# A graph attention kernel on one core: the attention output goes through DRAM two sequences at a time, its quotients come two slots later, and SyncE's queue is put in another order

## The chip, the core and the metric

The kernel runs on one core of a Trainium2 chip. The metric is the device time of one execution in microseconds (us), as the median of repeated runs. The engines named here are PE (TensorE, matrix products), DVE (VectorE), ACT (ScalarE), POOL (GpSimd) and SP (SyncE, which in this kernel issues every DMA). Each engine works through its own list of instructions in order. They meet at semaphores: an instruction that waits for a semaphore holds back all that stands behind it on its engine.

## What is computed

64 sequences of 128 tokens and 384 channels, 12 heads of 32 channels, float32. The reference, cut to its core:

```python
h = jnp.maximum(_layernorm(x, axis=-1), 0.0)
q = _split_heads(h @ Wq + bq); k = _split_heads(h @ Wk + bk); v = _split_heads(h @ Wv + bv)
scores = jnp.einsum('bhqd,bhkd->bhqk', q, k) / jnp.sqrt(HD)
scores = scores + beta * adj[:, None]
scores = jnp.where(adj[:, None] > 0, scores, -9e15)
probs = jax.nn.softmax(scores, axis=-1)
out = jnp.einsum('bhqk,bhkd->bhqd', probs, v)
return x + out.transpose(0, 2, 1, 3).reshape(B, N, D)
```

## The kernel before, in words

Four sequences make a group (`GROUP = 4`, 16 groups). The program is a row of **slots**, one for each sequence of each group, and all engines go through the same slots. Slot s (0 to 3) of a group works on several sequences at once: it projects q and k for the group, computes the scores of sequence a, transposes the probabilities of the sequence before it (e = a - 1), and finishes the output of the one before that (o = a - 2). The middle slots stand in a hardware loop of two groups a turn; the first and last groups are written out. The last six sequences (`F`) are finished in another way, by transposes on PE.

Three tiles are transposed in 32x32 blocks by DVE, which needs the blocks themselves moved between partitions. That is done through DRAM: one DMA writes 128 rows, a second set of four DMAs reads them back block by block. All three ways are on SP:

- the normalised input, two sequences at a time: `xhat_blocks` is written to `xhat_rows` in odd slots (384 KB), and read into `xhat_moved` in even slots by four DMAs;
- the first third of each sequence's probabilities: ACT's four exponentials fill `probs_blocks` (`exponentials_ahead`), SP writes it to `probs_rows` (256 KB) late in the slot, and in the next slot SP reads it into `probs_moved` by four DMAs of 64 KB. DVE then transposes it (`transpose_probs`), and PE multiplies it with v a slot later;
- the output: PE writes it transposed, DVE transposes the blocks into `out_blocks` (`store_outT`), SP writes it to `out_rows` (192 KB) and reads it into `out_moved` by four DMAs of 48 KB. One slot later DVE divides by the softmax's sum (`quotient`, into `y`), POOL adds x, and SP stores `y` to the output.

The order of each engine's work is written by hand in its `slot` function. DVE's in a slot of the loop: reciprocals, the 12 masking passes (`mask`; in slot 0 the next one stands before it), `store_outT`, the hidden state's transpose, `normalise` (xhat), `quotient`, `add_bv` (v), `transpose_probs`, then the statistics, the bias and the low part of the hidden state. SP's is in `slot(z)` of the sync block, and the change rewrites it. `LOADS` says which sequences of x are loaded in which slot, three groups ahead.

Of the kernel before, what the change touches and what calls it, by code (L numbers as in the profile page):

```python
# [29 lines left out]
HEADS = 12  # L30
GROUP = 4
# [10 lines left out]
LOADS = [[0], [1, 2], [3], []]  # L42
# [19 lines left out]
def gnn_attention(nc, x, adj, wq, bq, wk, bk, wv, bv, beta, out):  # L62
# [16 lines left out]
    with ExitStack() as ctx:  # L79
# [54 lines left out]
        rinv = sb("rinv", [P, 2, HEADS])  # L134
# [4 lines left out]
        THREE = KC * HD  # L139
# [53 lines left out]
        out_written = [sem(f"out_written{i}") for i in range(2)]  # L193

        class Slot:
# [14 lines left out]
            def __init__(self, i, off, s):  # L210
# [17 lines left out]
                before = 0 <= 4 * (n - 1) + s - 3 < FIRST_F  # L228
                self.moved, self.turned = [1] * before, [0] * (self.F and self.O and not self.L)
# [55 lines left out]
            def written(self, d):  # L285

                return 4 * self.i + (2 * (self.off - 1) + (self.s - 2 - d) // 2)
# [74 lines left out]
        def _(sp):  # L362
# [33 lines left out]
            def slot(z):  # L396
                if z.R:
                    sp.wait_ge(probs_rows_written, 16 * (z.e + 1))
                    for c in range(HC):
                        came = probs_rows[(z.s - 1) % 2, :, c * FOUR:(c + 1) * FOUR].rearrange("(r p) n -> p r n", r=HC)  # L400
                        goes = probs_moved[c * HD:(c + 1) * HD, (z.s - 1) % 2, :].rearrange("p (r n) -> p r n", r=HC)
                        sp.dma_start(goes, came).then_inc(probs_blocks_moved[(z.s - 1) % 2], 16)  # L402
# [4 lines left out]
                if not (z.static and not 1 <= z.groups(0) <= NG - 3):  # L407
                    if z.s % 2 == 1:
                        sp.wait_ge(xhat_ready, order(z.count(2)) + 1)
                        write_rows(z.s // 2)  # L410
                    if z.s == 2:
                        sp.wait_ge(rows_written[0], 16 * z.groups(0))
                        read_blocks(0)
                if z.M and z.s == 0:
                    sp.wait_ge(rows_written[1], 16 * z.groups(-1))
                    read_blocks(1)
                if z.Q:
                    sp.wait_ge(probs_ready[0], z.a + 1)
                    sp.dma_start(probs_rows[z.s % 2, :, :], probs_blocks[:, :]).then_inc(probs_rows_written, 16)  # L419
                if z.W:  # L420
                    sp.wait_ge(out_rows_written, 16 * (z.o + 1))
                    for b in range(HC):
                        came = out_rows[z.s % 2, :, b * THREE:(b + 1) * THREE].rearrange("(j p) n -> p j n", j=HC)
                        goes = out_moved[b * HD:(b + 1) * HD, z.s % 2, :].rearrange("p (j n) -> p j n", j=HC)
                        sp.dma_start(goes, came).then_inc(out_blocks_moved[z.s % 2], 16)  # L425
                for d in z.moved + z.turned:

                    sp.wait_ge(y_ready, z.o + 1 - d)
                    sp.dma_start(out[bass.ds(z.o - d, 1), :, :].rearrange("b t d -> t (b d)"),  # L429
                                 y[:, (z.s - d) % 2, :]).then_inc(out_written[(z.s - d) % 2], 16)  # L430
# [6 lines left out]
                if not (z.static and z.groups(3) >= NG):  # L437
                    if z.s == 0:


                        sp.wait_ge(stats_ready, z.count(1) + 2)
                    for q in LOADS[z.s]:
                        sp.dma_start(x_ring[:, bass.ds(z.ring(3, q), D)],  # L443
                                     x_v[:, bass.ds(z.groups(3), 1), q, :].rearrange("t g d -> t (g d)")).then_inc(x_loaded[(z.par + 1) % 2], 16)
                if z.L:
                    for m in range(KC):
                        sp.wait_ge(third_ready, m + 1)
                        sp.dma_start(out[z.o, :, m * P:(m + 1) * P], y[:, z.s % 2, m * P:(m + 1) * P]).then_inc(out_written[z.s % 2], 16)
# [3 lines left out]
            sp.wait_ge(out_written[0], 16 * B // 2)  # L452
            sp.wait_ge(out_written[1], 16 * (B // 2 + KC - 1))

        @block.gpsimd
        def _(pool):
# [25 lines left out]
            def slot(z):  # L482
# [11 lines left out]
                for d in z.moved + z.turned:  # L494
# [3 lines left out]
                    nc.gpsimd.tensor_tensor(y[:, z.s % 2 ^ d, :], y[:, z.s % 2 ^ d, :], x_ring[:, bass.ds(at, D)], ALU.add).then_inc(y_ready, 1)  # L498
# [131 lines left out]
        def _(dve):  # L630
# [68 lines left out]
            def store_outT(z):  # L699
                dve.wait_ge(pv_done, z.o + 1)  # L700
                if z.W:
                    if started(z.o):
                        dve.wait_ge(out_rows_written, 16 * z.o)
                    nc.vector.transpose(out_blocks[:, :].rearrange("p (b m d) -> p m b d", b=HC, m=KC),
# [6 lines left out]
            def reciprocals(z):  # L711
                dve.wait_ge(probs_ready[2], z.o + 1)
                if started(z.o - 1):
                    dve.wait_ge(normalised, z.o - 1)
# [347 lines left out]
```

## Time and profile before

| | |
|---|---|
| time before, median of 3 runs | 545.62 us (545.51 to 547.7) |
| the profiled execution's own time | 551.03 us |
| its span, first to last instruction | 548.9 us |
| busy: PE, DVE, ACT, POOL | 92%, 85%, 81%, 23% of the span |
| granted TensorE clock | 0.987 of full speed |
| DMA issues by SP in the output's way through DRAM | 58 writes, 232 reads |

The profile is of one execution. A page gives totals, the other views give instructions in order of time. Rows whose engine reads "SPq" are SP issuing DMAs: the duration is that of the issue, not of the transfer. "Idle before" in square brackets says how long the engine had nothing to do before an instruction and who ended that.

### The profile page before, as it was taken

To read this page: it belongs to the slowest core of one execution; us is meant where nothing else is said; L and a number is where in the kernel's file an instruction comes from. 1 tells how busy PE (TensorE), PEld (TensorE's weight loads), DVE (VectorE), ACT (ScalarE), POOL (GpSimd) and SP (SyncE) were. 2 spreads that over 40 slices of the span, in tenths; PEclk is the share of its full clock that TensorE was granted. 3 is DMA by queue.
4 is the path that set the end of the run, shared out by engine and by line. 5 is a ranking of instruction groups with operands and counts; after the bars stand their busy time and mean duration, and the time that the engine had idled before them with its cause. 6 is when DMAs were issued, how large, how long until landed. Compare 5 with 4: busy or idle time off the path is not lost.

```text
span 548.9 us, 17414 instructions
## 1 busy us (share of the span) xinstructions
PE 507.4 (92%) x5142; PEld 418.8 (76%) x5142; DVE 467.3 (85%) x2323; ACT 443.0 (81%) x1816; POOL 127.0 (23%) x204
## 2 busy tenths in 40 slices
PE   8897989997999989899899989999898998999986
PEld 7676868776878778688787878778786887888774
DVE  5686878978989798898989989898898998887796
ACT  3568596796988969788796988889698897989885
POOL 5412121222222222221222222122222221111121
PEclk9999999999999999999999999999899999999999
DMA  7516466776776777767687776767668566655311
GB/s 244 169 55 197 127 209 204 214 218 204 222 244 180 242 215 220 222 202 217 203 249 217 223 233 211 227 206 242 203 192 252 178 198 201 179 160 161 94 45 59
DMA packets 132840, 106.20 MB, mean 193 GB/s; under 512 B 44464, under 2 KB 121904, under 8 KB 132784
## 3 DMA queue, kind: packets, MB, share of 16 engines
q1 hardware_dynamic: 132784, 105.57, 63.5%
q8 instruction: 21, 0.34, 0.3%
q14 instruction: 35, 0.29, 0.2%
HBM read 55.84 MB, written 49.68 MB: 192 GB/s over the span
## 4 chain that ended last, share of the span: by engine, by line
SPq 38%; PE 19%; DMA 12%; DVE 10%; issue 8%; ACT 3%; DVEq 0%; ACTq 0%
SPq L425 12%; SPq L402 11%; DMA out_rows<-out_blocks 8%; PE G_ps L892 7%; PE S_ps L961 4%; SPq L429 4%; SPq L443 4%; PE S_ps L913 4%; SPq L394 4%; DMA probs_moved<-probs_rows 4%; DVE probs L726 4%; PE PT_ps L945 2%; PE PT_ps L929 2%; ACT probs_blocks L542 2%; SPq L419 1%
## 5 line engine op out<-in xcount | busy, mean ns | idle before, releaser
L527 ACT ACTIVATE probs<-probs,negmax 128x128 f32<-128x128 f32 x532 | 206.0, 397 | 0.0
L726 DVE CUSTOM_DVE_ANT_0 probs<-S_ps,bias 128x128 f32<-128x128 f32 x768 | 165.8, 284 | 14.4 <-PE S_ps L913 14.4
L542 ACT ACTIVATE probs_blocks<-probs,negmax 128x128 f32<-128x128 f32 x236 | 91.9, 393 | 71.9 <-DVE negmax L726 71.8
L498 POOL TENSOR_TENSOR y<-y,x_ring 128x384 f32<-128x384 f32 x63 | 63.9, 1014 | 299.6 <-DVE y L744 299.6
L892 PE MATMUL G_ps<-h_hi,w_hi 128*128 128x512 f32 x288 | 120.1, 417 | 0.0
L892 PE MATMUL G_ps<-h_hi,w_lo 128*128 128x512 f32 x288 | 119.0, 413 | 0.0
L892 PE MATMUL G_ps<-h_lo,w_hi 128*128 128x512 f32 x288 | 117.6, 408 | 0.0
L527 ACT ACTIVATION_READ_ACCUMULATOR probs<-probs,negmax 128x1 f32 x532 | 105.0, 197 | 0.0
L764 DVE STREAM_TRANSPOSE probsT<-probs_moved 128x512 f32<-128x512 f32 x59 | 41.8, 709 | 43.3 <-DMA probs_moved<-probs_rows 43.2
L913 PEld LDWEIGHTS S_ps<-qk 32*128 32x128 f32 x1536 | 50.9, 188 | 33.8 <-issue 32.3
L929 PE MATMUL PT_ps<-probsT,v 128*32 128x128 f32 x1512 | 55.6, 281 | 22.1 <-DVE probsT L764 10.7
L913 PE MATMUL S_ps<-qk 32*128 32x128 f32 x1536 | 63.9, 294 | 11.8 <-DVE h_lo L665 11.4
L550 ACT COPY probsT<-PT_ps 128x512 f32<-128x512 f32 x122 | 64.9, 579 | 6.9 <-PE PT_ps L945 6.3
L892 PEld LDWEIGHTS G_ps<-h_hi,w_hi 128*128 128x128 f32 x288 | 55.2, 192 | 15.1 <-issue 3.6
L945 PE MATMUL PT_ps<-ident,probs 128*128 128x128 f32 x492 | 66.2, 273 | 0.0
L961 PE MATMUL S_ps<-w_hi,h_hi 128*128 128x384 f32 x192 | 65.3, 340 | 0.0
L929 PEld LDWEIGHTS PT_ps<-probsT,v 128*32 128x32 f32 x1512 | 39.1, 111 | 34.3 <-issue 26.7
L892 PEld LDWEIGHTS G_ps<-h_lo,w_hi 128*128 128x128 f32 x288 | 55.1, 191 | 13.0 <-issue 3.2
L961 PE MATMUL S_ps<-w_hi,h_lo 128*128 128x384 f32 x192 | 64.6, 337 | 0.0
L961 PE MATMUL S_ps<-w_lo,h_hi 128*128 128x384 f32 x192 | 64.5, 336 | 0.0
L892 PEld LDWEIGHTS G_ps<-h_hi,w_lo 128*128 128x128 f32 x288 | 55.2, 192 | 11.6 <-issue 2.8
L726 DVE DVE_READ_ACCUMULATOR2_ANT negmax<- 128x1 f32 x768 | 63.8, 83 | 0.1
(60 smaller groups left out, 724.7 us busy)
## 6 DMA issues: line engine op xcount, KB each, us to landing
probs_rows<-probs_blocks SPq DMA_DIRECT2D x59, 256.0 KB, 2.8
probs_moved<-probs_rows SPq DMA_DIRECT2D x236, 64.0 KB, 2.3
out_dram<-y SPq DMA_DIRECT2D x63, 192.0 KB, 2.0
x_ring<-in_x_dram SPq DMA_DIRECT2D x61, 192.0 KB, 3.0
out_rows<-out_blocks SPq DMA_DIRECT2D x58, 192.0 KB, 2.1
out_moved<-out_rows SPq DMA_DIRECT2D x232, 48.0 KB, 2.1
xhat_rows<-xhat_blocks SPq DMA_DIRECT2D x26, 384.0 KB, 2.7
xhat_moved<-xhat_rows SPq DMA_DIRECT2D x104, 96.0 KB, 2.5
```

The lines of the kernel that those rows point to most:

```text
L402: sp.dma_start(goes, came).then_inc(probs_blocks_moved[(z.s - 1) % 2], 16)
L425: sp.dma_start(goes, came).then_inc(out_blocks_moved[z.s % 2], 16)
L498: nc.gpsimd.tensor_tensor(y[:, z.s % 2 ^ d, :], y[:, z.s % 2 ^ d, :], x_ring[:, bass.ds(at, D)], ALU.add).then_inc(y_ready, 1)
L527: last = nc.scalar.activation(p, p, ACT.Exp, bias=negmax[:, e, j * KC + m:j * KC + m + 1], scale=TURN, accum_out=rowsum[:, e, m * HC + j:m ...
L542: last = nc.scalar.activation(blocks[:, j, :, :], probs[:, a, j, 0, :].rearrange("p (c e) -> p c e", c=HC), ACT.Exp, bias=negmax[:, a, j * ...
L550: nc.scalar.copy(probsT[:, m, :], pT_bank(z, m)).then_inc(pT_stored[m], 1)
L726: last = nc.vector.tensor_tensor_reduce(probs[:, a, j, m, :], S_ps[:, j, m * N:(m + 1) * N], bias[(z.par + 1) % 2][:, z.s, :], 1.0, LARGES ...
L892: mm = nc.tensor.matmul(G_ps[:, u % 2, :], pairs[n][0], pairs[n][1], start=(n == 0), stop=(n == len(pairs) - 1))
L913: last = nc.tensor.matmul(S_ps[:, j, m * N:(m + 1) * N], qk_a[rs, m, ts], qk_a[rs, KC + m, ts], start=True, stop=True, tile_position=(j * ...
L929: last = nc.tensor.matmul(outT_ps[j * HD:(j + 1) * HD, m * N:(m + 1) * N], v[:, z.s % 2, h * HD:(h + 1) * HD], probsT[:, h // HC, h % HC * ...
L945: last = nc.tensor.transpose(pT_bank(z, m)[:, j * N:(j + 1) * N], probs[:, (z.s - 1) % 2, j, m, :], ident[:, :])
L961: last = nc.tensor.matmul(v_ps, hh, ww, start=(n == 0), stop=(n == len(pairs) - 1))
```

## The change

Five edits. (1) `out_blocks` and `out_rows` hold two sequences; SP writes and reads them in odd slots alone, so that there are half as many DMAs of twice the size (384 KB written, four reads of 96 KB). (2) The quotient, POOL's addition and the store to the output come two slots after the sequence's `store_outT` instead of one, with four places in `y` and `rinv`; `y` and `out_moved` now lie in `w_raw`, the raw weights' buffer, which is why the names in the lists below read `w_raw`. (3) In a slot SP issues the reads of the probabilities' blocks first, then the loads of x and of adj (`load_ahead`), which stood last; behind them come the ways of xhat, the write of the output pair, the write of the probabilities, the store of y, and the reads of the output pair. (4) x's sequences 2 and 3 of a group are loaded in slot 2, instead of 1 and 2 in slot 1. (5) At the first F slot two quotients fall due.

```diff
-LOADS = [[0], [1, 2], [3], []]
+LOADS = [[0], [1], [2, 3], []]
...
-        out_blocks = sb("out_blocks", [P, D])
-        out_rows = nc.dram_tensor("out_rows", [2, P, D], F32, kind="Internal").ap()
-        out_moved = sb("out_moved", [P, 2, D])
-        y = sb("y", [P, 2, D])
+        SIX = 2 * KC * HD
+        out_blocks = sb("out_blocks", [P, HC * SIX])
+        out_rows = nc.dram_tensor("out_rows", [2, P, HC * SIX], F32, kind="Internal").ap()
+        later = w_raw.rearrange("p k n -> p (k n)")
+        out_moved = later[:, 0:2 * HC * SIX].rearrange("p (i n) -> p i n", i=2)
+        y = later[:, 2 * HC * SIX:2 * HC * SIX + GROUP * D].rearrange("p (i n) -> p i n", i=GROUP)
...
-                before = 0 <= 4 * (n - 1) + s - 3 < FIRST_F
-                self.moved, self.turned = [1] * before, [0] * (self.F and self.O and not self.L)
+                first_f = n == NG and s == 0
+                self.moved = [2] * (not self.F and 4 * (n - 1) + s - 4 >= 0) + [2, 1] * first_f
+                self.turned = [0] * (self.F and self.O and not self.L)
...
             def slot(z):
                 if z.R:
                     sp.wait_ge(probs_rows_written, 16 * (z.e + 1))
...
                         sp.dma_start(goes, came).then_inc(probs_blocks_moved[(z.s - 1) % 2], 16)
-                if z.W:
-                    sp.wait_ge(outT_stored, z.o + 1)
-                    sp.dma_start(out_rows[z.s % 2, :, :], out_blocks[:, :]).then_inc(out_rows_written, 16)
+                load_ahead(z)
                 if not (z.static and not 1 <= z.groups(0) <= NG - 3):
...
+                if z.W and z.s % 2 == 1:
+                    sp.wait_ge(outT_stored, z.o + 1)
+                    sp.dma_start(out_rows[1 - z.s // 2, :, :], out_blocks[:, :]).then_inc(out_rows_written, 16)
                 if z.Q:
                     sp.wait_ge(probs_ready[0], z.a + 1)
                     sp.dma_start(probs_rows[z.s % 2, :, :], probs_blocks[:, :]).then_inc(probs_rows_written, 16)
-                if z.W:
-                    sp.wait_ge(out_rows_written, 16 * (z.o + 1))
+                for d in z.moved + z.turned:
+                    sp.wait_ge(y_ready, z.o + 1 - d)
+                    place = (z.s - 2 - d) % GROUP
+                    sp.dma_start(out[bass.ds(z.o - d, 1), :, :].rearrange("b t d -> t (b d)"), y[:, place, :]).then_inc(out_written[place], 16)
+                if z.W and z.s % 2 == 1:
+                    sp.wait_ge(out_rows_written, 16 * (z.pairs_written() + 1))
                     for b in range(HC):
...
-                for d in z.moved + z.turned:
...
-                if z.T and z.s == 1:
...
-                    for q in LOADS[z.s]:
...
             def store_outT(z):
                 dve.wait_ge(pv_done, z.o + 1)
                 if z.W:
-                    if started(z.o):
-                        dve.wait_ge(out_rows_written, 16 * z.o)
+                    if z.s % 2 == 0 and started(z.pairs_written()):
+                        dve.wait_ge(out_rows_written, 16 * z.pairs_written())
```

SP's list in the program, in the loop, from slot 1's write of the probabilities to slot 2's reads of them. Before (L419 is the write, L402 the reads, L425 the output's reads, L443 the loads of x):

```order
L419 DMA probs_rows<-probs_blocks 128x512
L425 DMA out_moved<-out_rows 32x4x96 x4
L429 ISA
L429 DMA out_dram<-y 128x384
L435 ISA
L435 DMA adj_in<-in_adj_dram 128x4x128
L443 ISA
L443 DMA x_ring<-in_x_dram 128x384
L443 ISA
L443 DMA x_ring<-in_x_dram 128x384
L398 REGISTER_ALU
L402 DMA probs_moved<-probs_rows 32x4x128 x4
```

And of the change, from the write of the output pair that stands just ahead of it:

```order
L440 DMA out_rows<-out_blocks 128x768
L442 REGISTER_ALU
L443 DMA probs_rows<-probs_blocks 128x512
L446 REGISTER_ALU
L448 ISA
L448 DMA out_dram<-w_raw 128x384
L450 ISA
L454 DMA w_raw<-out_rows 32x4x192 x4
L421 REGISTER_ALU
L425 DMA probs_moved<-probs_rows 32x4x128 x4
```

The three loads have left this stretch, and the output's reads (now L454) read what the write at the piece's head has only just brought to DRAM.

The next piece of SP's list, from slot 2's reads of the probabilities to its write of the next ones. Before:

```order
L402 DMA probs_moved<-probs_rows 32x4x128 x4
L406 DMA out_rows<-out_blocks 128x384
L412 REGISTER_ALU
L394 DMA xhat_moved<-xhat_rows 32x4x192 x4
L418 REGISTER_ALU
L419 DMA probs_rows<-probs_blocks 128x512
```

Of the change:

```order
L425 DMA probs_moved<-probs_rows 32x4x128 x4
L416 ISA
L416 DMA x_ring<-in_x_dram 128x384
L416 ISA
L416 DMA x_ring<-in_x_dram 128x384
L432 REGISTER_ALU
L401 DMA xhat_moved<-xhat_rows 32x4x192 x4
L442 REGISTER_ALU
L443 DMA probs_rows<-probs_blocks 128x512
```

The output's write is gone from an even slot, and two loads of x stand ahead of the write of the probabilities. On PE and ACT no instruction moves; on DVE and POOL only the quotient and the addition stand for another sequence, and two of each follow each other in the first F slot.

## Rows read from the trace of the kernel before

**Rows 1.** The page's head and its first part: busy time of each engine.

```profile
span 548.9 us, 17414 instructions
PE 507.4 (92%) x5142; PEld 418.8 (76%) x5142; DVE 467.3 (85%) x2323; ACT 443.0 (81%) x1816; POOL 127.0 (23%) x204
```

**Rows 2.** Waits of the engines, all of the span: us in total, times, longest.

```profile
DVE probsT L764 <- DMA probs_moved<-probs_rows: 43.2, 38, 2.7
```

**Rows 3.** The page's chain that ended last, by line.

```profile
SPq L425 12%; SPq L402 11%; DMA out_rows<-out_blocks 8%; PE G_ps L892 7%; PE S_ps L961 4%; SPq L429 4%; SPq L443 4%; PE S_ps L913 4%; SPq L394 4%; DMA probs_moved<-probs_rows 4%; DVE probs L726 4%; PE PT_ps L945 2%; PE PT_ps L929 2%; ACT probs_blocks L542 2%; SPq L419 1%
```

**Rows 4.** Timeline of DVE, one group of the loop: start, us, instruction, idle before.

```profile
269.50 0.70 DVE L764 STREAM_TRANSPOSE probsT<-probs_moved 128x512 f32<-128x512 f32 x1
...
275.56 0.55 DVE L744 TENSOR_TENSOR y<-out_moved,rinv 128x384 f32<-128x384 f32 x1
...
277.06 0.71 DVE L764 STREAM_TRANSPOSE probsT<-probs_moved 128x512 f32<-128x512 f32 x1 [0.48 <-DMA probs_moved<-probs_rows]
...
286.06 0.71 DVE L764 STREAM_TRANSPOSE probsT<-probs_moved 128x512 f32<-128x512 f32 x1 [1.92 <-DMA probs_moved<-probs_rows]
...
293.33 0.71 DVE L764 STREAM_TRANSPOSE probsT<-probs_moved 128x512 f32<-128x512 f32 x1 [0.21 <-DMA probs_moved<-probs_rows]
...
301.31 0.70 DVE L764 STREAM_TRANSPOSE probsT<-probs_moved 128x512 f32<-128x512 f32 x1
```

**Rows 5.** Timeline of SP in the same group: start, us of issuing, DMA.

```profile
275.97 0.36 SPq L386 DMA_DIRECT2D xhat_rows<-xhat_blocks  x1
276.81 0.32 SPq L419 DMA_DIRECT2D probs_rows<-probs_blocks  x1
277.48 1.82 SPq L425 DMA_DIRECT2D out_moved<-out_rows  x4
...
280.66 0.94 SPq L443 DMA_DIRECT2D x_ring<-in_x_dram  x2
281.72 1.78 SPq L402 DMA_DIRECT2D probs_moved<-probs_rows  x4
283.54 0.43 SPq L406 DMA_DIRECT2D out_rows<-out_blocks  x1
284.08 1.88 SPq L394 DMA_DIRECT2D xhat_moved<-xhat_rows  x4
286.08 0.36 SPq L419 DMA_DIRECT2D probs_rows<-probs_blocks  x1
...
289.62 2.05 SPq L402 DMA_DIRECT2D probs_moved<-probs_rows  x4
...
292.66 0.45 SPq L419 DMA_DIRECT2D probs_rows<-probs_blocks  x1
```

**Rows 6.** Timeline of POOL, slot 1 of the same group.

```profile
276.30 1.02 POOL L498 TENSOR_TENSOR y<-y,x_ring 128x384 f32<-128x384 f32 x1 [4.21 <-DVE y L744]
```

**Rows 7.** The page's DMA issues: count, size, median us from issue to landing.

```profile
probs_rows<-probs_blocks SPq DMA_DIRECT2D x59, 256.0 KB, 2.8
...
xhat_rows<-xhat_blocks SPq DMA_DIRECT2D x26, 384.0 KB, 2.7
xhat_moved<-xhat_rows SPq DMA_DIRECT2D x104, 96.0 KB, 2.5
```

**Rows 8.** Timeline of SP in a slot 1 soon after the start.

```profile
79.42 0.38 SPq L419 DMA_DIRECT2D probs_rows<-probs_blocks  x1
...
85.91 1.78 SPq L402 DMA_DIRECT2D probs_moved<-probs_rows  x4
```

**Rows 9.** Timeline of SP in the first slot 1 after the loop.

```profile
405.04 0.42 SPq L419 DMA_DIRECT2D probs_rows<-probs_blocks  x1
...
411.35 1.86 SPq L402 DMA_DIRECT2D probs_moved<-probs_rows  x4
```

**Rows 10.** Windows: busy us of each engine, clock, DMA share, GB/s.

```profile
105.00:398.00 293.00, 274.77 (x2828) 227.12 (x2827) 261.12 (x1308) 246.95 (x1021) 70.67 (x109) 0.99 0.73 219
...
452.00:484.00 32.00, 30.36 (x320) 25.39 (x319) 27.13 (x137) 28.33 (x119) 4.36 (x5) 1.00 0.63 191
```

More of the change, by code:

```diff
@@ L192, in gnn_attention @@
         third_normalised, third_ready = sem("third_normalised"), sem("third_ready")
-        out_written = [sem(f"out_written{i}") for i in range(2)]
+        out_written = [sem(f"out_written{i}") for i in range(GROUP)]
         class Slot:
@@ L394, in read_blocks, with load_ahead @@
                     sp.dma_start(goes, came).then_inc(blocks_moved[pair], 16)
[L396 to L402, printed above, removed]
-                if z.W:
-                    sp.wait_ge(outT_stored, z.o + 1)
-                    sp.dma_start(out_rows[z.s % 2, :, :], out_blocks[:, :]).then_inc(out_rows_written, 16)
[L407 to L419, printed above, removed]
-                if z.W:
-                    sp.wait_ge(out_rows_written, 16 * (z.o + 1))
[L422 to L425, printed above, removed]
-                for d in z.moved + z.turned:
-                    sp.wait_ge(y_ready, z.o + 1 - d)
-                    sp.dma_start(out[bass.ds(z.o - d, 1), :, :].rearrange("b t d -> t (b d)"),
-                                 y[:, (z.s - d) % 2, :]).then_inc(out_written[(z.s - d) % 2], 16)
+            def load_ahead(z):
                 if z.T and z.s == 1:
@@ L444, in slot @@
                                      x_v[:, bass.ds(z.groups(3), 1), q, :].rearrange("t g d -> t (g d)")).then_inc(x_loaded[(z.par + 1) % 2], 16)
+            def slot(z):
+                if z.R:
+                    sp.wait_ge(probs_rows_written, 16 * (z.e + 1))
+                    for c in range(HC):
+                        came = probs_rows[(z.s - 1) % 2, :, c * FOUR:(c + 1) * FOUR].rearrange("(r p) n -> p r n", r=HC)
+                        goes = probs_moved[c * HD:(c + 1) * HD, (z.s - 1) % 2, :].rearrange("p (r n) -> p r n", r=HC)
+                        sp.dma_start(goes, came).then_inc(probs_blocks_moved[(z.s - 1) % 2], 16)
+                load_ahead(z)
+                if not (z.static and not 1 <= z.groups(0) <= NG - 3):
+                    if z.s % 2 == 1:
+                        sp.wait_ge(xhat_ready, order(z.count(2)) + 1)
+                        write_rows(z.s // 2)
+                    if z.s == 2:
+                        sp.wait_ge(rows_written[0], 16 * z.groups(0))
+                        read_blocks(0)
+                if z.M and z.s == 0:
+                    sp.wait_ge(rows_written[1], 16 * z.groups(-1))
+                    read_blocks(1)
+                if z.W and z.s % 2 == 1:
+                    sp.wait_ge(outT_stored, z.o + 1)
+                    sp.dma_start(out_rows[1 - z.s // 2, :, :], out_blocks[:, :]).then_inc(out_rows_written, 16)
+                if z.Q:
+                    sp.wait_ge(probs_ready[0], z.a + 1)
+                    sp.dma_start(probs_rows[z.s % 2, :, :], probs_blocks[:, :]).then_inc(probs_rows_written, 16)
+                for d in z.moved + z.turned:
[4 more added lines that the diff above has]
+                    sp.wait_ge(out_rows_written, 16 * (z.pairs_written() + 1))
+                    for b in range(HC):
+                        came = out_rows[1 - z.s // 2, :, b * SIX:(b + 1) * SIX].rearrange("(j p) n -> p j n", j=HC)
+                        goes = out_moved[b * HD:(b + 1) * HD, 1 - z.s // 2, :].rearrange("p (j n) -> p j n", j=HC)
+                        sp.dma_start(goes, came).then_inc(out_blocks_moved[1 - z.s // 2], 16)
@@ L447, in slot @@
                         sp.wait_ge(third_ready, m + 1)
-                        sp.dma_start(out[z.o, :, m * P:(m + 1) * P], y[:, z.s % 2, m * P:(m + 1) * P]).then_inc(out_written[z.s % 2], 16)
+                        sp.dma_start(out[z.o, :, m * P:(m + 1) * P], y[:, GROUP - 1, m * P:(m + 1) * P]).then_inc(out_written[GROUP - 1], 16)
             slots(sp, slot)
-            sp.wait_ge(out_written[0], 16 * B // 2)
-            sp.wait_ge(out_written[1], 16 * (B // 2 + KC - 1))
+            for place in range(GROUP):
+                sp.wait_ge(out_written[place], 16 * (NG if place < GROUP - 1 else NG + KC - 1))
         @block.gpsimd
@@ L497, in slot @@
                     pool.wait_ge(normalised, z.o + 1 - d)
-                    nc.gpsimd.tensor_tensor(y[:, z.s % 2 ^ d, :], y[:, z.s % 2 ^ d, :], x_ring[:, bass.ds(at, D)], ALU.add).then_inc(y_ready, 1)
+                    place = back % GROUP
+                    nc.gpsimd.tensor_tensor(y[:, place, :], y[:, place, :], x_ring[:, bass.ds(at, D)], ALU.add).then_inc(y_ready, 1)
                 for q in z.stats:
```

38 lines of the change are left out of this document (21 added, 17 removed).

## The prediction

> **What bounds the kernel now.** I read the page's head first: PE is busy 92% of the span and DVE 85% [rows 1]. Neither can be read as full: a busy PE is pipelined work, and DVE has 82 us without work. The list of waits says where most of DVE's idle time lies: 43.2 us in 38 waits, all ahead of the transpose of the probabilities' blocks, for the DMA that moves them [rows 2]. The chain that ended last agrees from the other end: its largest parts are not an engine's work but SP's issues of the output's reads and of the probabilities' reads (L425 and L402, 12% and 11%), and the landing of the output's write (8%) [rows 3]. So the loop is bound by DVE's work and SP's queue in turn, and the change has to be worked out on SP's queue.
>
> The timeline of one group shows how. DVE's five transposes are 7.56, 9.00, 7.27 and 7.98 us apart, and waits of 0.48, 1.92 and 0.21 us stand before the middle three [rows 4]. The group is thus 31.81 us, of which 2.61 are waits and 29.20 DVE's own pace. The timeline of SP explains the long one [rows 5]. Slot 1 writes the probabilities at 276.81. Before it comes to reading them back, SP issues the output's four reads (1.82 us), the store of y, adj, and two loads of x, so that the reads begin at 281.72, 4.91 us after the write. After them come the output's next write and the xhat reads, so that slot 2's write is issued at 286.08, and its reads at 289.62. The transpose follows at 293.33. From slot 1's write to that transpose SP's row takes 4.91 + 4.36 + 3.54 + 3.71 = 16.52 us, and this row, not DVE, sets the pace over slots 2 and 3. From there to the next slot 1's write DVE sets it: no wait stands before the transpose at 301.31.
>
> **What the change removes, adds and moves.** Half of the output's writes and reads go (29 and 116 issues); at 0.46 us each (1.82 for four [rows 5]) that is 67 us of SP's issuing, 1.1 us a slot. Were SP's total the bound, that would be the gain; but only what stands on the 16.5 us row counts. Term by term, with the same group:
>
> (a) Slot 1's write to slot 2's reads, now 4.91. adj and the loads leave it. But the output's reads now wait for a write that is issued just ahead: xhat_rows goes at 275.97, 0.84 before the probabilities' write [rows 5], the output's pair right behind it, 0.4 before. The trace has no such pair. Its nearest row is the xhat write of the same 384 KB, 2.7 us to landing [rows 7]: the lower end. The upper end adds the transfer of the 384 KB ahead of it: the DMA engines moved 219 GB/s at 0.73 of their time [rows 10], so 300 GB/s in full, 1.3 us, together 4.0. I take 3.2, nearer to the lower end, since the median of 2.7 already holds other writes in flight and the one ahead has a start of 0.4. Then the output's reads are issued from 2.8 to 4.7 us after the probabilities' write, and the probabilities' reads at 4.75. Gain 0.16, between 0.65 and a loss of 0.65.
>
> The Trainium skill ("DMA: Bandwidth & Descriptors", Anatomy of one DMA) fits a DMA's time by 2.0 us plus its bytes over 436 KB a us, which gives 2.9 for 384 KB; its fit is for GpSimd's DMAs, the xhat row has 2.7 for SP's. By the page (a) would gain 0.46.
>
> (b) Slot 2's reads to its write, now 4.36: the output's write goes (284.08 - 283.54 = 0.54), two loads of x come in (281.72 - 280.66 = 1.06) [rows 5]: 4.88, a loss of 0.52.
>
> (c) Slot 2's write to slot 3's reads, now 3.54: the output's reads go. What is left is the landing of the write, 2.8 [rows 7]; the store of y fits inside it. 2.85, a gain of 0.69.
>
> (d) The reads to the transpose, 3.71 [rows 4, 5]: unchanged.
>
> Together 16.19 instead of 16.52: 0.33 a group here. In the loop's 293 us DVE was idle for 31.9 [rows 10], over 9.2 groups 3.5 each, 0.9 more than in the group shown; part of that is SP falling behind by more than here, and (a) and (c) then save more, since they end at a landing and not at an issue. I add a quarter of the 0.9 and take 0.55 a group, 5.0 us in the loop.
>
> Outside the loop two slots show a longer (a): 6.49 us soon after the start [rows 8] and 6.31 just behind the loop [rows 9]. At 4.75 they give back 1.7 and 1.6. In the other slots behind the loop, without loads, even slots gain (c) and odd slots lose some of it; PE was idle for only 1.64 us of 32 there [rows 10], so I take 1.0 for the whole part. In the first F slot a second quotient of 0.55 [rows 4] stands on DVE where each step waits for the last: 0.5 lost.
>
> Costed at nothing: slot 1's own transpose loses its wait (0.48), but slot 2's write then still waits for SP, so nothing follows. The wait of 1.92 shrinks by about 1 (the reads no longer land behind adj and loads), and nothing follows for the same reason. The quotient of slot 2 now needs the output's reads: the last is issued at 4.3 after the write and lands 2.5 later by the xhat reads of its new size [rows 7], at 283.6. DVE comes to it about 1.0 us before its transpose [rows 4], at 282.6: a new wait of 1.0 us. It hides inside what is left of the wait for the probabilities, which land at 285.1: quotient and v end at 284.6. POOL's addition ends 1.76 after the quotient's start [rows 4, 6], and its store is issued long before SP would need it in even slots; in odd ones SP waits longer for the output's write anyway.
>
> Sum: 5.0 + 1.7 + 1.6 + 1.0 - 0.5 = 8.8 us of the profiled execution's 551.03, which gives 542.2. That execution was 1% above the median of the runs, 545.62, so the forecast in their terms is 536.9, rounded to 537. The terms' own range is 532 to 542.9.
>
> **The rivals.** *SP's new wait makes it slower.* In odd slots the probabilities' reads are now queued behind a wait for a landing. If the output's pair lands only 4.0 us after its issue, (a) becomes 5.55, a loss of 0.64, and the row 16.99. Slot 3 suffers too. Its write at 292.66 moves 0.4 back behind the output's, and forward by 1.0 with slot 2's earlier transpose; reads 4.75 later and 3.71 to the transpose give 300.5, against DVE's own 300.8: 0.3 of slack, which 0.8 more use up, and 0.5 comes on top. That is 0.97 a group, 9 us, and the two slots outside give 1.6 less: 545.6 + 9 - 3 = 551. The point from which it decides: with (a) at 5.25, a landing of 3.7, the loop gains nothing. For it: two writes of 384 KB and one of 256 KB go out within 1 us. Against: adj and the loads now go out earlier. The Trainium skill (the same page and section) states that DMA engines don't wait on semaphores, the issuing sequencer does; by that rule all that is queued behind the output's reads waits. The 8% of the chain on that landing [rows 3] agrees. Chance 14%.
>
> *Nothing comes of it.* (b) loses what (c) gains, and (a) stands still with a landing of 3.4 to 3.7. Only the slots outside the loop are left, 0 to 3 us: 543 to 547. A repeat of this kernel tells 0.5%, 2.7 us, from no change at best. Chance 22%.
>
> *SP ceases to bind.* If landings shrink with less in flight, so that (a) is 3.5 and (b) and (c) hide, DVE's waits fall to 1 us a group: 2.5 x 9.2 = 23 us and 5 outside: 518. Against: the output's reads alone take 1.9 of (a) and their write 2.7. Chance 6%; and 8% for something between it and my range, 525 to 532, by a landing of 2.7.
>
> **How the numbers follow.** My forecast has 50%. Faster by over 0.5% is 50 + 6 + 8 = 64%, the same 22%, slower 14%. The range reaches from 530 (landing 2.7: 0.5 a group more) to 549 (most of the first rival). It leaves out some 15%.
>
> **What the profile would show.** Right: in the loop the probabilities' reads come 4.5 to 5.0 us after the write in odd slots and 2.8 to 3.0 in slot 2; SP waits for out_rows some 2 us in each odd slot; a new DVE wait before the quotient of slot 2; DVE's wait for probs_moved near 30 us instead of 43.2; groups of 31.3. Wrong: reads at 5.3 or more, or a wait before slot 0's transpose, where none is now; or the quotient's wait so long that the transpose is no longer the last to be served.

## The result, and the profile after

The change made the kernel slower by half a per cent: 549.98 us median of 20 runs (547.62 to 553.56) against 547.38 us of the kernel before, run beside it 20 times (545.17 to 549.6). The ratio is 1.005, with a 95% interval of 1.003 to 1.007. The profiled execution spans 550.4 us, 1.5 more than [rows 1].

The page's head and first part, of the changed kernel:

```profile
span 550.4 us, 17259 instructions
PE 504.8 (92%) x5142; PEld 417.6 (76%) x5142; DVE 469.1 (85%) x2323; ACT 443.3 (81%) x1816; POOL 127.4 (23%) x204
...
DMA out_rows<-out_blocks 14%; SPq L425 12%; DMA probs_rows<-probs_blocks 10%; SPq L454 7%; PE G_ps L906 7%; SPq L401 6%; PE S_ps L975 4%; SPq L416 3%; DMA probs_moved<-probs_rows 3%; PE S_ps L927 2%; DVE probs L737 2%; PE PT_ps L959 2%; PE PT_ps L943 2%; SPq L393 1%; ACT probs L538 1%
```

The engines' work is as it was. The chain has changed: against [rows 3] the issues of the output's reads (now L454) fell from 12% to 7%, but the landing of the output's write rose from 8% to 14%, and the landing of the probabilities' write, which was not in the list, has 10%. SP's issuing was replaced by SP's waiting.

DVE's waits of the changed kernel, all of the span, against [rows 2]:

```profile
DVE probsT L778 <- DMA probs_moved<-probs_rows: 24.2, 30, 2.9
...
DVE w_raw L757 <- issue: 8.8, 11, 1.9
...
DVE out_blocks L715 <- DMA out_rows<-out_blocks: 3.7, 2, 2.7
DVE w_raw L757 <- DMA w_raw<-out_rows: 3.5, 2, 2.1
```

DVE waits 19 us less for the probabilities' blocks. Against that, 12.3 us of waits before the quotient are new (L757; by the program it is the output's reads that it waits for there, also where the view says "issue"), and 3.7 for the output's buffer.

SP's own waits in a stretch of the loop, 144 to 398 us. Before:

```profile
SPq L419 <- ACT probs_blocks L542: 8.6, 14, 1.1
SPq L425 <- DMA out_rows<-out_blocks: 8.5, 14, 1.0
SPq L386 <- DVE xhat_blocks L654: 1.1, 3, 0.4
SPq L406 <- DVE out_blocks L704: 1.0, 1, 1.0
```

After:

```profile
SPq L425 <- DMA probs_rows<-probs_blocks: 26.4, 16, 2.0
SPq L454 <- DMA out_rows<-out_blocks: 20.9, 16, 2.0
SPq L393 <- DVE xhat_blocks L665: 3.4, 2, 2.1
SPq L448 <- POOL w_raw L509: 1.7, 6, 0.4
```

This is the view that tells most. Before, SP waited for ACT's exponentials in 14 slots: there it was on time, and ACT and DVE set the pace. After, there is not one wait for ACT: SP comes late to the probabilities' write in every slot. Yet it spends 47 us waiting for its own writes to land, against 8.5 before, and only 5.1 us waiting for DVE and POOL. What half the issues saved went into those waits, and hardly a slot is left in which SP has time in hand.

The timeline of SP over one group's slots 1 and 2, in the changed kernel, beside [rows 5]:

```profile
309.89 0.36 SPq L393 DMA_DIRECT2D xhat_rows<-xhat_blocks  x1
310.30 0.42 SPq L440 DMA_DIRECT2D out_rows<-out_blocks  x1
310.90 0.38 SPq L443 DMA_DIRECT2D probs_rows<-probs_blocks  x1
...
314.14 1.74 SPq L454 DMA_DIRECT2D w_raw<-out_rows  x4
315.99 1.79 SPq L425 DMA_DIRECT2D probs_moved<-probs_rows  x4
317.99 0.96 SPq L416 DMA_DIRECT2D x_ring<-in_x_dram  x2
319.09 2.03 SPq L401 DMA_DIRECT2D xhat_moved<-xhat_rows  x4
321.34 0.34 SPq L443 DMA_DIRECT2D probs_rows<-probs_blocks  x1
...
324.30 1.75 SPq L425 DMA_DIRECT2D probs_moved<-probs_rows  x4
```

The pair's write goes at 310.30, and SP can read it only from 314.14, 3.8 us later. The probabilities' reads follow at 315.99, 5.09 after their write; the next write is issued 5.35 after that, its reads 2.96 later.

The timeline of DVE in the same group, beside [rows 4]:

```profile
303.66 0.70 DVE L778 STREAM_TRANSPOSE probsT<-probs_moved 128x512 f32<-128x512 f32 x1
310.65 0.71 DVE L778 STREAM_TRANSPOSE probsT<-probs_moved 128x512 f32<-128x512 f32 x1
317.69 0.56 DVE L757 TENSOR_TENSOR w_raw<-w_raw,rinv 128x384 f32<-128x384 f32 x1 [0.33 <-issue]
319.32 0.71 DVE L778 STREAM_TRANSPOSE probsT<-probs_moved 128x512 f32<-128x512 f32 x1 [0.60 <-DMA probs_moved<-probs_rows]
327.69 0.71 DVE L778 STREAM_TRANSPOSE probsT<-probs_moved 128x512 f32<-128x512 f32 x1 [1.31 <-DMA probs_moved<-probs_rows]
335.67 0.70 DVE L778 STREAM_TRANSPOSE probsT<-probs_moved 128x512 f32<-128x512 f32 x1
```

The group takes 32.01 us, where the one of [rows 4] took 31.81. The wait of slot 1 is gone, that of slot 2 is split between the quotient and the transpose, and that of slot 3 has grown from 0.21 to 1.31.

Where the time went, read from three transposes (the first, the twelfth, the forty-fourth of 59) on DVE's timeline. Before:

```profile
39.84 0.70 DVE L764 STREAM_TRANSPOSE probsT<-probs_moved 128x512 f32<-128x512 f32 x1
...
139.63 0.70 DVE L764 STREAM_TRANSPOSE probsT<-probs_moved 128x512 f32<-128x512 f32 x1
...
397.80 0.70 DVE L764 STREAM_TRANSPOSE probsT<-probs_moved 128x512 f32<-128x512 f32 x1
```

After:

```profile
38.67 0.70 DVE L778 STREAM_TRANSPOSE probsT<-probs_moved 128x512 f32<-128x512 f32 x1
...
143.76 0.70 DVE L778 STREAM_TRANSPOSE probsT<-probs_moved 128x512 f32<-128x512 f32 x1
...
399.63 0.70 DVE L778 STREAM_TRANSPOSE probsT<-probs_moved 128x512 f32<-128x512 f32 x1
```

The first eleven slots take 105.1 us instead of 99.8, the next 32 (eight groups of the loop) 255.9 instead of 258.2. So in these two executions the steady loop gained, 0.29 us a group, and the early part lost 5.3.

The granted clock of TensorE has a part in both numbers. In the changed kernel it fell from 2.4 GHz to 1.2 GHz twice ahead of the end of the loop. A window ahead of the first fall, in which PE has no instruction, and one behind it (the number behind POOL's column is the clock):

```profile
132.00:134.00 2.00, 0.00 (x0) 0.00 (x0) 0.00 (x0) 2.00 (x7) 0.00 (x0) 1.00 0.79 267
136.00:142.00 6.00, 5.70 (x36) 4.79 (x35) 5.19 (x31) 1.41 (x8) 0.59 (x1) 0.50 0.54 147
```

TensorE had been idle for 3.33 us before that fall. The slot with the low clock, the last of the early eleven, took 9.75 us; slots of its kind in the loop mostly take 7.98. The kernel before has two such stretches in its early part and two in its 32 slots of the loop, where the change has one and one. The second of its two in the loop lies in the last of the 32 slots, which took 8.86 us, where those of its kind at full clock take 7.98 to 8.33. Up to 0.9 of the 2.3 us gained in the loop can be this.

### The profile page after: what moved, and what is told of

Its sections match the earlier page's. It is cut to its first block, busy times and chain, and to the rows that moved or that the text cites. A ratio compares the mean times of both kernels' runs of the same rounds, so it can differ in the third digit from the quotient of the medians.

```text
span 550.4 us, 17259 instructions
## 1 busy us (share of the span) xinstructions
PE 504.8 (92%) x5142; PEld 417.6 (76%) x5142; DVE 469.1 (85%) x2323; ACT 443.3 (81%) x1816; POOL 127.4 (23%) x204
## 4 chain that ended last, share of the span: by engine, by line
SPq 30%; DMA 27%; PE 18%; DVE 8%; issue 7%; ACT 1%; DVEq 0%
DMA out_rows<-out_blocks 14%; SPq L425 12%; DMA probs_rows<-probs_blocks 10%; SPq L454 7%; PE G_ps L906 7%; SPq L401 6%; PE S_ps L975 4%; SPq L416 3%; DMA probs_moved<-probs_rows 3%; PE S_ps L927 2%; DVE probs L737 2%; PE PT_ps L959 2%; PE PT_ps L943 2%; SPq L393 1%; ACT probs L538 1%
## 5 line engine op out<-in xcount | busy, mean ns | idle before, releaser
L509 POOL TENSOR_TENSOR w_raw<-w_raw,x_ring 128x384 f32<-128x384 f32 x63 | 64.0, 1017 | 312.7 <-DVE w_raw L757 312.7
```

The lines of the kernel that those rows point to most:

```text
L509: nc.gpsimd.tensor_tensor(y[:, place, :], y[:, place, :], x_ring[:, bass.ds(at, D)], ALU.add).then_inc(y_ready, 1)
```

## The experiments

Two theories stood against each other for the loss. **Theory 1**, the landing: the output's pair is written behind xhat's 384 KB, lands late, and SP waits for it in front of the probabilities' reads. **Theory 2**, the order: loads that stood behind the writes now stand ahead of slot 2's write and make it late. Means below are over the eight groups between the twelfth and forty-fourth transpose, from the issue times and landings in each kernel's timeline. Every ratio is to the kernel before, run beside that experiment. Where a time is set against the change, the change's 549.98 us is of another session; the kernel before had medians of 547.32 to 547.99 us in all of them.

**e1, the order alone.** The kernel before, with `LOADS` and SP's loads as in the change:

```diff
-LOADS = [[0], [1, 2], [3], []]
+LOADS = [[0], [1], [2, 3], []]
...
                         sp.dma_start(goes, came).then_inc(probs_blocks_moved[(z.s - 1) % 2], 16)
+                if z.T and z.s == 1:
...
+                    for q in LOADS[z.s]:
...
                 if z.W:
                     sp.wait_ge(outT_stored, z.o + 1)
```

> The kernel before with SP's new order and LOADS alone; the output still goes by single sequences, quotients one slot later. Theory 1 (the pair's landing, for which SP now waits in odd slots, eats the gain): without the pair the order should show its own worth, faster than before by 0.5 to 1.5%, since the probabilities' reads no longer stand behind the loads. Theory 2 (the loads ahead of slot 2's write of the probabilities lose it; in the trace of the change reads to next write is 5.11 us in slot 2 instead of 4.34): slower than before by 0.5% or more, since the pair's saving of issues is missing too.

554.57 us median, ratio 1.012 (1.007 to 1.016). The order alone loses. Slot 2's reads to its write rose from 4.34 to 5.53 us, as Theory 2 has it; slot 1's write to its reads fell from 5.06 to 4.23, not enough. But this is not all of the loss: of the 5.2 us by which this trace is longer, 1.3 lie in the 32 slots and 3.3 in the 15 behind them, where the last of x is loaded at 415 us of 554. And two of the 32 slots took 10.1 us, where those of their kind mostly take 7.98, at a mean granted clock of 0.66; TensorE had been idle for 2.55 and 1.71 us before. What lengthened the last slots was not tried.

**e2, the pairs alone.** The change with SP's old order:

```diff
-LOADS = [[0], [1], [2, 3], []]
+LOADS = [[0], [1, 2], [3], []]
...
                         sp.dma_start(goes, came).then_inc(probs_blocks_moved[(z.s - 1) % 2], 16)
-                load_ahead(z)
+                if z.W and z.s % 2 == 1:
+                    sp.wait_ge(outT_stored, z.o + 1)
+                    sp.dma_start(out_rows[1 - z.s // 2, :, :], out_blocks[:, :]).then_inc(out_rows_written, 16)
...
+                for d in z.moved + z.turned:
+                    sp.wait_ge(y_ready, z.o + 1 - d)
...
+                load_ahead(z)
```

> The change with SP's old order and LOADS: the pair's write behind the probabilities' reads, its reads straight behind the probabilities' write, y and loads last. Theory 1: the same as before or slower (the landing wait is still in front of the probabilities' reads, and adj and two loads stand behind it again: slot 1's write to the reads 6 us or more). Theory 2: faster than before by 1% (half the issues, no loads ahead of the write).

538.6 us, ratio 0.984 (0.979 to 0.989). The pairs with the later quotients gain 1.6%. The pair, written as the first thing after the probabilities' reads, lands after 2.4 us. SP's waits in the same stretch of e2:

```profile
SPq L429 <- DVE out_blocks L715: 23.1, 16, 1.9
SPq L442 <- ACT probs_blocks L553: 10.4, 15, 1.1
...
SPq L448 <- DMA out_rows<-out_blocks: 5.4, 10, 0.6
```

SP is on time again: it waits for ACT in 15 slots and has 23 us in hand before the pair's write. So Theory 1's form in which the pair is harmful in itself is out; the product of e1 and e2 is 0.996, and the change is at 1.005. The intervals of e1 and e2 are half a per cent each way, so that a loss from the two together is likely but not certain from these two runs. What the two together do is put the pair behind xhat's write (e4) and loads ahead of slot 2's write (e3).

**e3, the loads of even slots in the landing's shadow.** The change, but:

```diff
-                load_ahead(z)
+                if z.s % 2 == 1:
+                    load_ahead(z)
...
                     sp.dma_start(out[bass.ds(z.o - d, 1), :, :].rearrange("b t d -> t (b d)"), y[:, place, :]).then_inc(out_written[place], 16)
+                if z.s % 2 == 0:
+                    load_ahead(z)
```

> The change with the loads of even slots behind the store of y, where SP otherwise waits 2 us for the probabilities' write to land; odd slots as in the change. Theory 2 (loads ahead of the write): reads to write in slot 2 falls from 5.1 to 4.1 us, nothing is lost elsewhere, 1.0 us a group in 9 groups and some outside: 1.5 to 2% faster than the change, 1 to 1.5% faster than before. Theory 1: the odd slots' wait for the pair stays at 5 us, but it is the same row, so also a gain; only if the loads now delay the reads' landing (2.3 instead of 1.55 us) does the gain fall under 0.5%.

531.59 us, ratio 0.972 (0.968 to 0.976), 3.3% faster than the change (531.59 / 549.98). Slot 2's reads to its write fell from 5.11 to 3.80, and its write to slot 3's reads from 2.84 to 2.40, although two loads stand there now. The gain is twice what was expected from 1 us a group. Part of that is slot 0, whose load the same edit moves: its reads to its write fell from 4.63 to 3.86.

**e4, the pair's write ahead of xhat's.** The change, but:

```diff
                 load_ahead(z)
+                if z.W and z.s % 2 == 1:
+                    sp.wait_ge(outT_stored, z.o + 1)
+                    sp.dma_start(out_rows[1 - z.s // 2, :, :], out_blocks[:, :]).then_inc(out_rows_written, 16)
                 if not (z.static and not 1 <= z.groups(0) <= NG - 3):
```

> The change with the output pair's write ahead of the xhat write in odd slots. Theory 1: the pair lands 0.7 to 1 us sooner, as in the kernel before (2.1 us for a write that nothing stands ahead of, 3.3 now), so probabilities' write to reads in odd slots falls from 4.9 to about 4.2 us: 0.5 to 1% faster than the change. Theory 2: the same as the change within 0.3%.

532.32 us, ratio 0.973 (0.969 to 0.978), 3.2% faster than the change. The same two DMAs changed places and nothing else. The probabilities' write to their reads fell from 4.97 to 4.16 in slot 1 and from 4.83 to 4.23 in slot 3. The sooner landing is the smaller part of it in slot 1: there the pair lands 3.35 us after its issue instead of 3.63 (the loads still go out ahead of it), but it is issued 1.42 instead of 0.54 us ahead of the probabilities' write. In slot 3 it lands after 2.55 instead of 3.21 and is issued 0.97 instead of 0.47 us ahead. SP's waits for the pair in the stretch, 20.9 us above, are almost gone in e4:

```profile
SPq L425 <- DMA probs_rows<-probs_blocks: 25.3, 16, 2.0
...
SPq L454 <- DMA out_rows<-out_blocks: 3.3, 7, 0.7
```

Both theories are thus right, each for about 3%, though all that had to be explained was a loss of 0.5%: the change holds a gain of several per cent and two faults that eat it. Neither edit's gain is a matter of the clock: neither trace has a stretch at 1.2 GHz in its 32 slots, which take 244.7 and 245.7 us instead of 255.9, and the one that the change has there costs it some 0.7.

**e5, two buffers for the probabilities' blocks.** In the change ACT waits 10.0 us for the probabilities' write to land, as `probs_blocks` is single. The buffer is doubled:

```diff
-                if started(z.a):
-                    act.wait_ge(probs_rows_written, 16 * z.a)
+                if started(z.a - 1):
+                    act.wait_ge(probs_rows_written, 16 * (z.a - 1))
```

> The change with probs_blocks double, so that ACT's four exponentials of a sequence need not wait for the write of the sequence before to land. Theory A (a late write holds up ACT through the single probs_blocks, which makes the next write late too; this is why the first 130 us lose 5 us and why small delays of SP cost so much): ACT's 10.0 us of waits for probs_rows go, the stretch of the first eleven transposes falls from 105 to about 97 us, 1 to 1.8% faster than the change. Theory B (it is SP's queue with its landing waits alone that sets the pace; ACT's waits are a by-product): within 0.3% of the change, ACT's waits gone all the same.

549.97 us, ratio 1.003 (1.000 to 1.007): the change's own time. ACT's waits for `probs_rows` fell from 10.0 us in 6 to 3.8 us in 2, but the first eleven slots still take 104.3 us (in a traced execution of 555.51 us, 1% above that median). Theory A fell, Theory B stands: ACT's wait was a by-product of SP's late write.

**e6, the old split of the loads.** The change with `LOADS = [[0], [1, 2], [3], []]`.

> The change with the old split of the loads, x's sequences 1 and 2 in slot 1 and 3 in slot 2: one load less ahead of slot 2's write, one more in slot 1, where SP has about 0.5 us to spare before it waits for xhat. If the loads ahead of slot 2's write are what costs (half of what the loads behind the store gave, 3.3%): reads to write in slot 2 falls from 5.1 to 4.6 us and the time by 0.8 to 1.6% against the change. If what counts is SP's sum over the group or the bytes ahead of the odd slot's writes: same as the change, or slower by up to 1%, since slot 1's pair of writes then lands behind a second load.

558.08 us, ratio 1.018 (1.012 to 1.024), 1.5% slower than the change. Slot 2's reads to its write did fall, 5.11 to 4.49. But the second load in slot 1 stands ahead of the three writes: the pair of slot 1 lands 4.48 us after its issue instead of 3.63, and the reads come at 5.85 instead of 4.97. The load more in slot 1 cost 0.88 us there, the load less in slot 2 gave 0.62.

**e7, the output's halves apart.** Written one sequence a slot, read in pairs:

```diff
-                if z.W and z.s % 2 == 1:
+                if z.W:
                     sp.wait_ge(outT_stored, z.o + 1)
-                    sp.dma_start(out_rows[1 - z.s // 2, :, :], out_blocks[:, :]).then_inc(out_rows_written, 16)
+                    half = slice(z.s % 2 * KC * HD, (z.s % 2 + 1) * KC * HD)
+                    sp.dma_start(out_rows[1 - z.s // 2, :, :].rearrange("p (b n) -> p b n", b=HC)[:, :, half],
+                                 out_blocks.rearrange("p (b n) -> p b n", b=HC)[:, :, half]).then_inc(out_rows_written, 16)
```

> The change with the output written to DRAM one sequence a slot (192 KB, 384-byte runs, at the pair's place in SP's list) and only read back in pairs. It adds an issue of 0.45 us in even slots ahead of the probabilities' write, and takes 192 KB off the odd slots' burst of writes. If the landing of 384 KB behind 384 KB is what costs: the output's write lands after about 2.9 instead of 3.4 to 3.7 us, probabilities' write to reads in odd slots 4.3 instead of 4.9: faster than the change by 0.5 to 1.5%. If the count of issues ahead of a write is what costs: slower than the change by 0.5%.

566.54 us, ratio 1.035 (1.029 to 1.041), the slowest of all. In slot 1 the write lands hardly sooner (3.45 us instead of 3.63; 3.10 instead of 3.21 in slot 3), and the reads come 0.26 sooner; but the one issue more in an even slot, ahead of the probabilities' write, raised slot 2's reads to its write from 5.11 to 5.64 and slot 0's from 4.63 to 5.24. Its groups take 33.3 us (266.7 / 8) instead of 32.0. The issue ahead of a late write cost more than its own 0.45 us. Some of the 10.9 us that the 32 slots are longer than the change's is the clock: five of them have a stretch at 1.2 GHz, one in the change. Those five took 8.61 to 9.51 us, where slots of their kind at full clock take 7.98 to 8.06, and TensorE had been idle for 1.45 to 2.39 us before each. So SP's delays can cost twice, once as idle time and once as slow matrix products behind it. What is behind the rest was not taken apart (the write's runs are 384 bytes here, and they sit in the same slot as the xhat reads).

**e8, both mends.** e3's and e4's edits in one kernel.

> Both mends together: the loads of even slots behind the store of y, and the pair's write ahead of the xhat write. Each alone took 10 us off the loop's stretch of 256 us and brought it to 245. DVE's own pace there is 29.2 us a group, 8 groups, 234 us. If the two effects add (SP still sets the pace at 245): 236 to 239 us for the stretch, 525 us in all, 4% below before. If DVE and its waits for PE already set it: 243 us or more and 530 us in all.

523.21 us, ratio 0.954 (0.950 to 0.959): 4.6% faster than the kernel before, 4.9% faster than the change (523.21 / 549.98), and 1.6% faster than e3. The stretch of 32 slots takes 240.6 us, 30.1 a group, between the two expectations and above DVE's 29.2. SP's waits of e8 in the same window:

```profile
SPq L449 <- POOL w_raw L512: 12.4, 25, 0.8
SPq L431 <- DVE out_blocks L718: 11.6, 9, 1.5
SPq L444 <- ACT probs_blocks L556: 9.9, 15, 0.9
SPq L393 <- DVE xhat_blocks L668: 4.9, 13, 0.5
SPq L425 <- DMA probs_rows<-probs_blocks: 2.2, 3, 1.2
SPq L457 <- DMA out_rows<-out_blocks: 2.1, 4, 0.6
...
```

39 us of waiting for engines, 4 for landings: the picture of the change turned round. What sets the pace now is TensorE. Between 144 and 372 us PE is busy for 226.95 of 228 us, against 216.13 in the change, and the chain that ended last runs over PE's instructions for all but 0.5% of it. A better order of SP's queue can therefore hardly gain more in this loop. The timeline of SP in e8 shows the loads in the shadow of a landing:

```profile
297.35 0.36 SPq L444 DMA_DIRECT2D probs_rows<-probs_blocks  x1
298.21 0.36 SPq L449 DMA_DIRECT2D out_dram<-w_raw  x1
298.90 0.93 SPq L416 DMA_DIRECT2D x_ring<-in_x_dram  x2
300.48 1.76 SPq L425 DMA_DIRECT2D probs_moved<-probs_rows  x4
```

**e9, slot 1's loads behind the store.** The change, with adj and slot 1's load of x (`load_ahead` for `z.s == 1`) behind the store of y; slot 2's stay.

> The change with slot 1's loads alone (adj, 256 KB, and one sequence of x, 192 KB) moved from behind the probabilities' reads to behind the store of y, where SP waits for the pair to land; slot 2's loads stay ahead of its write. If bytes in flight ahead of the odd slot's writes make the pair land late: the pair in slot 1 lands after 3.0 to 3.2 us instead of 3.7, probabilities' write to reads 4.4 instead of 5.0 us, 0.5 to 1.5% faster than the change. If only issues ahead of a write and the place behind the xhat write count: same as the change within 0.3%, or slower, since the issues now stand in front of the output's reads.

543.91 us, ratio 0.993 (0.990 to 0.996), 1.1% faster than the change. The pair in slot 1 lands after 3.00 us instead of 3.63, the reads come at 4.69 instead of 4.97. That sooner landing is the bytes' share of Theory 1. The 1.1% are not the bytes' alone, though: the two issues left from ahead of slot 1's write too, whose distance from the reads before it fell from 4.51 to 3.86 us.

**e10, all loads behind the store.** e8 with slot 1's loads behind the store too.

> Both mends and slot 1's loads behind the store of y too. If bytes ahead of the writes still count: 0.3 to 1% faster than both mends alone (4.6% below before). If the loop is by now DVE's (SP waits for ACT, DVE and POOL there; the stretch is 240.6 us against DVE's 234), the same within 0.3%, or slower where the issues delay the output's reads, which the quotient of the next slot waits for.

525.18 us, ratio 0.960 (0.957 to 0.963). The pair now lands after 2.4 us in both odd slots, but slot 1's reads come at 4.35 instead of 3.74, and adj and the load stand in front of the output's reads: no gain over e8, 0.4% more, which the intervals don't part. With TensorE busy throughout in e8 there was little left to gain. e8 is the best version here.

## Why the prediction was wrong

**What held.** The row on which the sum was made held. From slot 1's write to slot 3's transpose I forecast a gain of 0.33 us for the group shown; the mean over seven groups of the loop fell from 16.74 to 16.37, 0.37. The terms, in means over eight groups: (a) 5.06 to 4.97, where I had 4.91 to 4.75; (b) 4.34 to 5.11, a loss of 0.77 where I had 0.52; (c) 3.68 to 2.84, a gain of 0.84 where I had 0.69, and 2.84 itself is the 2.85 forecast; (d) 3.64 to 3.40, a gain of 0.24 where I had none, which I put down to the reads no longer landing behind a load. The quotient's new wait in slot 2 came, inside the wait for the probabilities as said.

**The size that was off.** The pair's landing, taken as 3.2 us between 2.7 and 4.0, was 3.63 in slot 1 and 3.21 in slot 3. Two causes have numbers: without xhat's 384 KB directly ahead it is 3.35 and 2.55 (e4), without the loads ahead of those 3.00 in slot 1 (e9), with one load more 4.48 (e6). The formula of the Trainium skill ("DMA: Bandwidth & Descriptors", Anatomy of one DMA) gives 2.9 us for 384 KB. The traces have 2.34 and 2.40 in e2, where only the probabilities' reads go ahead of the pair, and 4.48 in e6; the formula has no term for what is in flight.

**The step that failed** is the sentence "From there to the next slot 1's write DVE sets it". I took the part of the group from slot 3's transpose to the next slot 1's write as DVE's, and therefore as unchanged, and gave slot 3's landing wait 0.3 us of slack. That was not quite so even before. The chain that ended last, over this part of the group of [rows 4] and of the changed kernel's group shown above (pieces that reach over an edge count in full):

```profile
by line: DVE probs L726 14.7%; DMA out_rows<-out_blocks 13.4%; SPq L425 11.5%; SPq L402 10.9%; issue 10.6%; ACT probs_blocks L542 9.6%; PE S_ps L913 7.4%; DVE probsT L764 4.7%; DVE h_lo L665 3.7%; SPq L443 3.6%; DVE bn L638 2.9%; SPq L429 2
by line: DMA out_rows<-out_blocks 46.4%; SPq L425 20.4%; DMA probs_rows<-probs_blocks 16.3%; issue 11.1%; SPq L401 10.4%; SPq L454 10.3%; SPq L416 6.8%; SPq L408 3.7%; SPq L393 2.2%; SPq L356 0.9%; SPq L429 0.3%; SPq L435 0.2%; SPq L414 0.2
```

Before, engines and SP's queue share it: DVE, ACT and PE have the pieces up to SP's write at 301.40, SP's issues and a landing those behind it. In the changed kernel it is issues and landings from end to end, and no engine's instruction is on it. SP is late in slots 3, 0 and 1 too: no wait for ACT in the stretch at all. The mean of that part rose from 15.46 to 15.65 in the loop, which takes half of the 0.37 (a small rise, where single groups of the change go from 15.2 to 16.5). In the two groups before those, whose slot-1 writes are the sixth and the tenth of the 59, it rose from 15.44 to 18.11, while the forecast row stood still (18.32 and 18.37). Between 118 and 128 us, too, the chain has nothing but SP's issues and landings. Of these 5.3 us, 4.9 lie ahead of the twelfth transpose, nearly all that the early part lost, and where I had credited 1.7 for one slot; 1.8 of them are the slot with the low clock. The mirror of it is e8: there SP has slack, and the same two numbers are 15.24 and 15.72, and the first eleven slots take 91.2 us.

The signs that I had put down would hardly have told. The reads came at 4.97 us on the mean (5.3 or more in two groups of eight), slot 2's at 2.84, a wait stands before the quotient, and before slot 0's transpose only one of 0.22 us in eight. They all look at single waits; SP has no time in hand in any slot, and that shows in none of them. Groups are 32.0 us and not 31.3.

The slots after the loop gave back 0.75 us (116.0 to 115.3 over the last 15 transposes) where I had 2.6. The loss in the first F slot was 0.4 to 0.5 as forecast (the last transpose to the end: 35.1 and 35.6).

**The rivals.** The first rival, SP's new wait, is the mechanism: it was put at a landing of 3.7 us, where the loop gains nothing, and 3.63 and 3.21 came, with a loop that gains next to nothing. Its sum of 551 was near the measured 549.98, but that is luck in part: the loss came in the early part, not in the loop, and the sum takes off 3 us for what is outside the loop, where its own terms leave 2.2 (3.8 less 1.6), so that it should have read 552. I gave it 14% because I priced the wait on one row, and did not see that the queue would have no slot left to catch up. The rule that the prediction cites there from the Trainium skill ("DMA: Bandwidth & Descriptors", Anatomy of one DMA), that the waiting for a semaphore happens on the issuing sequencer and not in the DMA engines, agrees with the trace: 47.3 us of landing waits in a stretch of 254. But landing waits are only dear when nothing else is left to be issued in them: e3 puts loads into one and gains 3.3%.

**What stays open.** Why the early slots suffer so much more than the loop from the same order; the low clock explains 1.8 us of it, and itself follows on idle time. Their landings are longer (the probabilities' write of slot 1 4.9 us on the mean against 3.75), and SP's own issues stall there at times (one of 3.12 us for four DMAs, where 1.74 is usual). Three issues take over 1.5 us each in the early part, at 65.9, 100.2 and 126.0 us, and a packet of 16 KB on an instruction queue stands within 0.6 us of the start of each. That the one causes the other was not tried. In the timeline of SP of the changed kernel one wait for the pair is 5.7 us from its issue:

```profile
78.05 0.42 SPq L440 DMA_DIRECT2D out_rows<-out_blocks  x1
78.58 0.37 SPq L443 DMA_DIRECT2D probs_rows<-probs_blocks  x1
79.20 0.94 SPq L448 DMA_DIRECT2D out_dram<-w_raw  x1
83.73 1.74 SPq L454 DMA_DIRECT2D w_raw<-out_rows  x4
```

Such stalls stand in the trace before too; my reading is that SP had slack then to catch up and has none after, which e8 supports and e5 doesn't contradict (it excludes ACT's single buffer). What lengthens the landings was not tried.

## What to carry to other kernels

An engine that issues all DMAs in order is a resource like any other: count, over a whole period, its issues and the landings it waits for, slot by slot, and ask in which slots it still waits for an engine. Where none is left, it sets the pace everywhere, however small each delay looks on one path. A delay that leaves TensorE idle can cost a second time, if its clock falls behind it. A landing wait in such a queue is free time for issues that nobody is waiting for: put loads behind a write, not ahead of it, and keep bytes that are not urgent from leaving just ahead of a write whose landing is waited for. Halving the number of DMAs is worth something only if the larger ones don't land later in front of someone who waits.

## What was not expected of the hardware

A write of 384 KB landed 2.4 us after its issue when only the 256 KB of the probabilities' reads went just ahead of it (e2, e10), 3.2 behind another write of 384 KB (the change, slot 3), 3.63 with 448 KB of loads before both (slot 1), 3.35 with these loads and without the other write (e4), and 4.48 with 640 KB of loads and the other write (e6). The last load of 192 KB thus cost 0.85 us of landing.
